# TensorE products of constants in seven pauses of a four-layer attention and expert kernel

## The reference, cut to what matters

```python
x = _L0_conv_ref(x, ...)    # per image: softmax(q.T k) over 256 positions, 16-wide q and k; Wf, batch norm, relu
x = _L1_conv_ref(x, ...)    # sigmoid gate from mean(Q * K), V * gate, softmax over 16, added to x
t = _to_tokens(x)
t = t + _L2_attn_ref(_ln_t(t), ...)   # 8 heads of 16, over the 8 images at each position
t = t + _L2_ffn_ref(_ln_t(t), ...)    # 8 experts of 512, gelu, the best two by softmax
t = t + _L3_attn_ref(_ln_t(t), ...)   # 8 heads of 16, over the 256 positions of each image
t = t + _L3_ffn_ref(_ln_t(t), ...)    # 8 experts of 256, silu(x w1) * (x w3), the best two
x = _from_tokens(t, x)
```

## Time and profile before

| | us |
|---|---|
| median of 3 runs | 695.27 |
| lowest, highest | 694.11, 695.28 |
| the profiled execution, whole | 695.18 |
| its span, first to last instruction | 693.4 |
| PE busy | 608.5 |
| DVE busy | 540.9 |
| mean granted PE clock | 0.818 |

### The profile page before, as it was taken

One profiled execution on the slowest core, in us unless ns is written; L12 is line 12 of the kernel. 1 busy time (PEld: TensorE's weight loads), 2 busy tenths in 40 slices (PEclk: granted clock), 3 DMA queues, 4 the chain that ended last, 5 costly groups with the idle time before them and its releaser, 6 DMA issues. The chain is left out here.

```text
span 693.4 us, 9974 instructions
## 1 busy us (share of the span) xinstructions
PE 608.5 (88%) x3188; PEld 493.8 (71%) x3188; DVE 540.9 (78%) x1142; ACT 401.5 (58%) x787; POOL 148.2 (21%) x114
## 2 busy tenths in 40 slices
PE   7896865987799999999997988888865889999996
PEld 3784664976678888887886777677744668888874
DVE  2638459982977787878788798899977779999987
ACT  3522221102578888888773698888863445555553
POOL 0094036952611011102011021111103011111100
PEclk9697567989699999999998555555555899999999
DMA  4000000001042202221000000000001032222211
GB/s 174 1 0 1 0 1 0 1 1 61 1 155 92 91 1 92 91 91 46 16 0 1 1 2 0 0 0 0 1 2 45 5 144 84 85 84 95 87 61 45
DMA packets 9699, 28.78 MB, mean 42 GB/s; under 512 B 960, under 2 KB 3264, under 8 KB 9536
## 3 DMA queue, kind: packets, MB, share of 16 engines
q1 hardware_dynamic: 9664, 28.34, 12.0%
HBM read 27.15 MB, written 1.18 MB: 41 GB/s over the span
## 5 line engine op out<-in xcount | busy, mean ns | idle before, releaser
L1225 DVE TENSOR_TENSOR hL<-hraw,hH 128x1024 fp32r<-128x1024 f32 (+1 forms) x128 | 131.1, 1050 | 35.9 <-ACT hH L991 35.3
L1059 PE MATMUL ps<-xH,wH 128*128 128x512 f32 x256 | 103.3, 404 | 1.7 <-DVE xL L1130 1.1
L995 ACT ACTIVATE hraw<-ps,bias 128x512 f32<-128x512 f32 x128 | 86.8, 686 | 29.0 <-PE ps L1061 24.5
L1061 PE MATMUL ps<-xH,wL 128*128 128x512 f32 x256 | 102.6, 401 | 0.0
L1060 PE MATMUL ps<-xL,wH 128*128 128x512 f32 x256 | 102.5, 401 | 0.0
L926 POOL TENSOR_TENSOR wL<-wraw,wH 128x1024 fp32r<-128x1024 f32 (+1 forms) x16 | 36.0, 2251 | 239.0 <-DVE wH L1111 239.0
L1073 PE MATMUL ps<-hH,wH 128*128 128x512 f32 x192 | 76.2, 397 | 6.6 <-DVE hL L1225 6.6
L1075 PE MATMUL ps<-hH,wL 128*128 128x512 f32 x192 | 76.0, 396 | 0.0
L1074 PE MATMUL ps<-hL,wH 128*128 128x512 f32 x192 | 75.5, 393 | 0.0
L1000 ACT ACTIVATE hraw<-ps 128x512 f32<-128x512 f32 x64 | 38.4, 600 | 51.4 <-PE ps L1061 49.8
L991 ACT ACTIVATE hH<-hraw 128x1024 fp32r<-128x1024 f32 x64 | 67.5, 1055 | 1.0
(11 more groups left out here) (234 smaller groups left out, 1212.7 us busy)
## 6 DMA issues: line engine op xcount, KB each, us to landing
G<-gates_scratch SPq DMA_DIRECT2D x32, 512.0 KB, 4.7
wraw<-in_ex SPq DMA_DIRECT2D x8, 514.5 KB, 5.6
wraw<-in_ex SPq DMA_DIRECT2D x8, 384.0 KB, 4.9
w<-in_pack SPq DMA_DIRECT2D x1, 1420.5 KB, 8.1
xs<-in_x SPq DMA_DIRECT2D x4, 256.0 KB, 4.7
out<-acc SPq DMA_DIRECT2D x4, 256.0 KB, 2.1
w<-in_pack SPq DMA_DIRECT2D x1, 501.0 KB, 3.7
gates_scratch<-gT SPq DMA_DIRECT2D x4, 32.0 KB
```

Of the source, the lines that this page charges most:

```text
L995: act.activation(hraw[:, k % 2, h, :], ps[:, h, :], ACT.Gelu, bias=bias[:, place(k, last)[0], h:h + 1]).then_inc(z["act"], 1)
L1059: pe.matmul(o, wH[:, p, at:at + P], xa, start=True, stop=False)
L1061: x = pe.matmul(o, wL[:, p, at:at + P], xa, start=False, stop=True)
L1225: dve.tensor_tensor(hL[:, k % 2, g * half:(g + 1) * half, :], src, hi.bitcast(F32), ALU.subtract).then_inc(z["hl"], 1)
```

## The change

`keep_busy` issues n matmuls of f32 with the identity matrix as one operand and the first 512 columns of the packed weights as the other, 128 rows in, 512 columns out, into a PSUM bank that holds nothing needed at that point. No one reads what they write, and no semaphore is raised. They stand in PE's list at seven places:

- layers 0 and 1: two ahead of `transposes(0)`, after a wait for ACT's four exponentials of pair 0, whose bank they use; and five ahead of `energies1(0)`
- attention of layer 2: two between `keys_bias(0)` and the first `ln_transposes`; and three between `final_bias(1)` and `sums(1)`, after a wait for ACT's copy of half 0's sums (`ot`), whose bank they use
- experts of layer 2: two after the first `ln_transposes`, one after the logits of the first half, two after those of the second. The semaphore `lgp` is still raised by the last logits product
- experts of layer 3: two between the transposes of t and the first `ln_transposes`

```diff
@@ in the first block's PE list; the second helper, for the later blocks, is the same with ps[:, bank, :]
+            def keep_busy(bank, n):
+
+                for _ in range(n):
+                    pe.matmul(bank, ident, w[:, 0:CH], start=True, stop=True)
...
             def transposes(p):
+                if p == 0:
+                    pe.wait_ge(m["ex"], 4)
+                    keep_busy(bank(0, 0), 2)
                 pe.wait_ge(m["an"], p + 1)
...
             def energies1(p):
+                if p == 0:
+                    keep_busy(bank(0, 1), 5)
                 pe.wait_ge(m["vd"], p + 1)
...
             keys_bias(0)
+            keep_busy(pe, OTB2, 2)
             ln_transposes(pe, 0, m2["ltp"], 0, LB2, 4)
...
             final_bias(1)
+            pe.wait_ge(m2["ot"], 1)
+            keep_busy(pe, OTB2, 3)
             sums(1)
             final(1)
...
                 LGB = 6
+                if layer == 1:
+                    keep_busy(pe, 0, 2)
                 for s in range(S):
                     ln_transposes(pe, nn, gs["ltp"], s)
                     if layer == 1 and s == 0:
                         pe.wait_ge(fin["done"], NCH)
+                    if layer == 0 and s == 0:
+                        keep_busy(pe, 5, 2)
                     if layer == 0 or s == 1:
...
+                    if layer == 0:
+                        keep_busy(pe, 5, 1 + s)
                 x.then_inc(gs["lgp"], 1)
```

More of the change, by code:

```diff
@@ L497, in add_bias, with keep_busy @@
                 pool.tensor_tensor(ts, ts, wc(name)[:, None].to_broadcast([P, B, P]), ALU.add).then_inc(done, 1)
+        def keep_busy(pe, bank, n):
+            for _ in range(n):
+                pe.matmul(ps[:, bank, :], ident, w[:, 0:CH], start=True, stop=True)
         def flat(banks):
```

## The result

The changed kernel takes **686.90 us** (median of four runs, 685.41 to 688.42) against 694.69 us of the kernel before in the same comparison (four runs, 693.87 to 695.28): a ratio of 0.9889, 95% interval 0.9856 to 0.9921. The time is inside the range, 1.4 us under the forecast of 688.3. The profiled execution took 685.83 us (span 683.9, 693.4 before), so the two traces differ by 9.5 us, and the medians by 7.8. In the comparisons of this document runs more than 1.5% above the fastest of their kernel are left out of the ratio; that happened in one kernel of the experiments only, where five of twelve runs took 702 to 715 us, and there the ratio understates the loss.

What follows compares the result with a forecast made beforehand. The prediction took the granted TensorE clock (1.2 or 2.4 GHz), where something waits for it, as what counts; 0.7 + 1.2 + 3.0 + 0.6 + 1.5 = 7.0 us off the 695.27 us median gave 688.3 us, range 685.2 to 692.4.

Steps and rivals of the forecast that it cites:

- two before L263: Layers 0 and 1, before transposes L263: earlier clock rise, partly absorbed by GpSimd's gaps; 0.7 us gained (0 to 0.8).
- five before L298: Layers 0 and 1, pause before L298: nothing delayed, level lost later in the open rest; 0 us (0 to 2).
- two after the bias: Layer 2's attention: level still lost before queries L627, but their low part shrinks; 1.2 us gained (0 to 3.0).
- three before L672: Layer 2's attention, before the second sums: level held over the pause; 3.0 us gained (0 to 3.0).
- layer 2's prologue: Layer 2's expert prologue, 2 + 1 + 2 products: path to the gates is DVE's; 0 (1.3 lost to 0.3 gained).
- layer 3's prologue, L506: Layer 3's expert prologue: level up by transposes L506, which take 1.0 us less; 0.6 us gained (0 to 0.6).
- the same, the gates: Layer 3's expert prologue: a shift keeps the level over the 2.22 us pause before gates L1039; 1.5 us (0 to 1.5).
- The low end of the range: Whole kernel: the lucky layer 1 case with the second attention never low, 1.8 us more gained; some 685.2 us.
- the signs that I had named: Right: second L672 14.5 us, L263 done by 34.5, layer 3's gates 1.9. Wrong: L672 low, or products outlasting DVE's release.
- only the pause before L672 pays: Rival, chance 0.22: of all places only the one before the second sums gains, 3.0 us; total 692.3 us.
- luck in layer 1 as well: Rival, chance 0.25: level also kept after layer 3's load wait, up to 1.9 us more; 8.9 us gained, total 686.4.
- slower: Rival, chance 0.04: products don't hold the level, L672 keeps 17.43 us, L1059 starts late; 1.5 to 3.1 us lost, 697.4.

Runs made afterwards that it cites:

- the single run: Only the place under discussion added to the kernel before: three products before the second L672, ratio 0.9959; for L298, both first-layer places (2 + 5), ratio 0.9974.
- only before the sums: Only the three products ahead of the second L672 in layer 2's attention added to the kernel before: 690.79 us, ratio 0.9959.
- only after the bias: Only the two products after the first bias of layer 2's attention added to the kernel before: 690.45 us, ratio 0.9950.
- only prologues: Only the products in the two expert prologues (2 + 1 + 2 in layer 2, two in layer 3) added to the kernel before: 693.33 us, ratio 1.0000.
- only one before the sums: One product instead of three ahead of the second L672, nothing else added to the kernel before: 694.59 us, ratio 1.0002.

## Why the prediction was right, and where not

The forecast of 7.0 us is near the 7.1 to 7.8 us measured, but it is a sum in which some terms were too small and others didn't exist, so it is in good part luck that the total is this near. The terms, with what the pair of traces shows and what the timed kernels show:

| term | forecast | traces | timed |
|---|---|---|---|
| two before L263 | 0.7 | 0.84 | 1.8 with the next |
| five before L298 | 0 | 0.45 | |
| two after the bias | 1.2 | 3.3 | 3.5 |
| three before L672 | 3.0 | 2.9 | 2.8 |
| layer 2's prologue | 0 | 0 | 0.0 with the next |
| layer 3's prologue, L506 | 0.6 | 0.35 | |
| the same, the gates | 1.5 | 0 | |
| start of layer 3's attention | not listed | about 1.5 | |

**Three before the second L672: right, by its own steps.** Start at 1.00 and 14.53 us for 17.43; the single run gives the same. That I took the upper bound because 0.5 us open is far below all lost pauses is confirmed from the other side: 2.43 us open lose everything.

**Two before L263: near, and in part by chance.** I had the start of the next work rounded to GpSimd's gaps: L263's successors gained 1.65 us at 34, and L298 only 0.84 at 62.5, against 0.7 to 0.8 forecast. But the execution alone accounts for up to 1.5 us in L263 and for 1.0 us in L298's start (62.50 to 63.53 with nothing added), and the means over seven executions each are only 0.36 us apart. So the agreement of 0.84 with 0.7 is largely chance; that GpSimd's gaps do the rounding was argued from one L413 and wasn't tested by itself.

**Five before L298: too small.** I had the mechanism (the level is lost later, "0 to 2: part of the 7.01 us of L298") and wrote 0, since L298's 16-column products were called small. They are not clock-free: 6.32 us for 7.01 in the changed kernel and 6.13 in the single run, 0.7 to 0.9 us of which 0.45 arrives. Over all seven executions with these products it is 5.32 to 7.01, so in one of them nothing was gained.

**Two after the bias: the step that failed.** It reads "More than 2.2 us stay open, so the level is still lost before the queries", and then took a mean rise of 3.5 us from the queries on. I had priced the bias at the level of the profile (1.95 us) and the products at either (1.8 or 3.6). Even so 5.10 less 3.6 is 1.5 us and not "more than 2.2", less than any pause that I had seen lose the level. And at 1.2 GHz, as in eight of the fourteen profiles, the bias alone takes 3.75 and the products 3.78: nothing stays open, dense work begins ahead of the queries instead of with them, and the rise is over when they start. That is my own upper bound (3.0, "never low"), and I should have seen that the two cases are one question: at which level the bias runs. The trace with the level up shows my forecast's case, 2.05 us open and queries of 3.53 us. The rise of 6.05 us, the longest in my list, was also counted too late: from 93.91, though the eight transposes of L506 ran from 91.26 and only 0.69 us were open between. As the level rises within such transposes in the changed kernel (at 90.58), they belonged to the dense work.

**The gates of layer 3: a gain that wasn't there.** I argued that the pause of 2.22 us was near the edge and any shift could keep the level. Near the edge it is not: in all four profiled executions with a pause of 2.18 to 2.25 us the gates were slow (3.40 to 3.48 us), three of them with the products of this prologue; fast gates stood behind shorter pauses, 1.12 or 1.13 us for the most part, because the up products ahead had run low. No shift by the change decides that: six of eight profiles without any product there have the gates at 1.91 us. The earlier trace rows had caught a poor execution. The kernel with the prologues alone measures 1.0000. The 0.6 us of the transposes L506 show in the trace (1.10 us for 1.97), but by 1.0000 nothing of them arrives that could be measured.

**The start of layer 3's attention** gained 1.5 us between the traces, which the forecast doesn't have. It isn't the change's: from the first L1544 of the attention to the next layer norm (L489) the trace of before took 157.35 us and the changed kernel's 155.37, but four kernels with nothing added in or near this stage (only before the sums, only after the bias, only prologues, only one before the sums) took 155.33 to 155.37 as well. The trace of before had a low stretch at the start of the stage (373.02 to 376.44) that these have not. It is the execution, as far as these runs tell. By the same reading, the 9.5 us between the two traces hold some 2 us of this luck, and the medians' 7.8 and 7.2 us are the better measure.

So the two main errors, 2.3 us too little after the bias and 1.5 to 2.1 too much in layer 3, all but cancelled. The low end of the range was added up wrongly: 686.4 less 1.8 is 684.6, not 685.2; the measured time lies above both. Of the signs that I had named, the second L672, L263's end (34.04), L298's start and the queries came as for "right"; layer 3's gates (3.42 us) did not, and a product that still ran when DVE's release had come, named as a sign of "wrong", occurred twice and cost nothing. The rivals: "only the pause before L672 pays" is out, by the run with the two products after the bias above all (0.9930 to 0.9970); "luck in layer 1 as well" didn't occur in that place (the stretch after the load is low in both); "slower" is out, yet its mechanism is real with other products (one row) and in another place (layer 3's attention).

## What to carry to other kernels

Products of constants in a pause pay when they close it on the path that sets the end: count the open rest at both clock levels of the work ahead of it. Give them the full 128 rows: here 128 held the level and one did not, and nothing between was tried in a pause. A stage bounded by other engines gained nothing here from a full clock, and the filler there cost double whenever the level was down. Before a term rests on the level in one profiled execution, compare the same place in other executions of the same code: in this kernel it moved by 1 to 2 us of work where nothing was changed.

## What the runs showed of the hardware

- Products of one row let the level fall while PE is busy (3.03 of 3.45 us, 0.83 in the table); with 128 rows, of about the same length (2.84 us), the sums behind them started at 1.00.
- Transposes alone raise it: within the 32 of L263 at 35.10 us in the trace of before, at 33.01 in another execution of the same code.
- The gain from filling a pause is no straight line in the number of products: 0.0 us for one and 2.8 for three ahead of the sums. After the bias it was 0.6 for one and 3.5 for two, where the interval of the first reaches from a loss of 1.0 us to a gain of 2.2.
- Filler is shorter when the clock is high, and so fills less: with the bias at 2.4 GHz two products left 2.05 us open and the queries behind them ran at 1.2 GHz; with the bias at 1.2 GHz they left none, and the queries ran at 2.4.
- The moments at which the level changes differ between executions of unchanged code (the 32 transposes of L263 took 5.14 to 6.64 us). The times go with it: of the 80 executions of the kernel before that stand beside the experiments, the 23 with a mean clock of 0.824 or more took 691.7 to 692.8 us, and the 24 with 0.818 or less took 693.3 to 698.9.
